# Graph layer 0 of a two-layer network: the order of two copies on ACT, the last tile's own rows, and the order of the last two tiles on DVE

## The reference

```python
h  = maximum(layernorm(x), 0)
xp = (h @ W).reshape(N, 4, 256)                 # with a_src, a_dst: one score per node and head
e  = leaky_relu(a_src[src] + a_dst[dst], 0.2)   # edges and self loops
ee = exp(e - segment_max(e, dst)[dst]); z = segment_sum(ee, dst)
out = segment_sum(xp[src] * (ee / z[dst]), dst)
x  = x + relu(out + bias)
h  = maximum(layernorm(x), 0)                   # the input of layer 1, and its two scores al, ar
```

## Time and profile before

| what | value |
|---|---|
| time, median of 3 runs | 2076.7 us (2073.75 to 2079.98) |
| time of the profiled execution | 2076.24 us |
| its span, first to last instruction | 2074.9 us (1.3 us less) |
| mean granted PE clock | 0.834 of full |
| busy: PE, DVE, ACT, POOL | 79%, 55%, 19%, 70% |
| gathers of `attend` (line 928), landing, min/median/max | 4.2/6.9/13.1 us |

### The profile page before, as it was taken

One profiled execution on the slowest core, in us unless ns is written; L12 is line 12 of the kernel. 1 busy time (PEld: TensorE's weight loads), 2 busy tenths in 40 slices (PEclk: granted clock), 3 DMA queues, 4 the chain that ended last, 5 costly groups with the idle time before them and its releaser, 6 DMA issues. The chain is left out here.

```text
span 2074.9 us, 27577 instructions
## 1 busy us (share of the span) xinstructions
PE 1642.4 (79%) x10226; PEld 913.5 (44%) x10226; DVE 1137.7 (55%) x2762; ACT 400.0 (19%) x766; POOL 1454.1 (70%) x1331
## 2 busy tenths in 40 slices
PE   5882998896067779787688787853799999999995
PEld 2441444442044445454444444531355555555554
DVE  4874777875026666676666666662344334443331
ACT  2220221211011212212122122111222222222221
POOL 3687888787677777777777777605777777777730
PEclk9996999998557677676777777766799999999998
DMA  6331323321399999999999999727999999999961
GB/s 212 101 91 34 87 80 113 97 79 54 134 357 303 337 335 346 353 321 327 350 338 345 337 340 352 262 76 293 408 409 409 410 409 409 407 410 407 406 227 46
DMA packets 187999, 560.54 MB, mean 270 GB/s; under 512 B 46439, under 2 KB 51252, under 8 KB 187604
## 3 DMA queue, kind: packets, MB, share of 16 engines
q0 software_dynamic: 140832, 416.41, 54.8%
q1 hardware_dynamic: 43428, 129.15, 18.9%
q10 hardware_dynamic: 3600, 13.16, 1.6%
HBM read 553.70 MB, written 53.27 MB: 293 GB/s over the span
## 5 line engine op out<-in xcount | busy, mean ns | idle before, releaser
L928 POOL DMA_INDIRECT ring<-layer_rows,idx x360 | 390.7, 1085 | 122.2 <-issue 106.2
L1494 POOL DMA_INDIRECT ring<-layer_rows,idx x360 | 361.9, 1005 | 116.6 <-issue 108.5
L414 POOL DMA_INDIRECT src_lists<-pay_T,slot_T x266 | 336.5, 1265 | 95.5 <-issue 83.8
L510 PE MATMUL mm<-w_sb,hT 128*128 128x512 f32 x800 | 360.1, 609 | 0.0
L1060 PE MATMUL acc<-ring,weight 128*32 128x256 f32 (+1 forms) x3600 | 331.0, 488 | 5.3 <-DVE weight L1167 5.2
L510 PEld LDWEIGHTS mm<-w_sb,hT 128*128 128x128 f32 x800 | 155.4, 197 | 187.4 <-issue 187.4
L1556 PE MATMUL acc<-ring,weight 128*32 128x512 f32 x1600 | 202.4, 625 | 35.4 <-ACT weight L1504 35.4
L1011 PE MATMUL turned<-ident,edge_a 128*16 128x128 f32 (+1 forms) x125 | 39.8, 319 | 217.6 <-ACT score_T L953 144.3
L1060 PEld LDWEIGHTS acc<-ring,weight 128*32 128x32 f32 (+1 forms) x3600 | 149.4, 138 | 127.6 <-issue 86.4
L1132 DVE TENSOR_REDUCE highest<-wide 128x4 f32<-128x512 f32 x125 | 86.2, 690 | 172.6 <-PE wide L1027 170.6
L1589 PE MATMUL mm_l<-w_high,hT_high 128*128 128x512 f32 x400 | 165.7, 414 | 1.8 <-DVE y L1664 1.8
(11 more groups left out here) (233 smaller groups left out, 2277.0 us busy)
## 6 DMA issues: line engine op xcount, KB each, us to landing
layer_rows<-row_l ACTq DMA_DIRECT2D x25, 514.0 KB, 3.7
layer_rows<-row_l SPq DMA_DIRECT2D x25, 514.0 KB, 7.2
own<-layer_rows SPq DMA_DIRECT2D x25, 512.0 KB, 8.8
x<-xb SPq DMA_DIRECT2D x25, 512.0 KB, 6.3
x1t<-x SPq DMA_DIRECT2D x25, 512.0 KB, 9.3
xt<-in_x_dram SPq DMA_DIRECT2D x24, 512.0 KB, 5.2
xb<-in_x_dram SPq DMA_DIRECT2D x24, 512.0 KB
out_dram<-y SPq DMA_DIRECT2D x24, 512.0 KB
```

The source lines that it names most:

```text
L414: pool.indirect_dma_start(out=list_d, out_offset=bass.IndirectOffsetOnAxis(ap=slot_T[:, b:b + 1], axis=0), in_=pay_T[:, b:b + 1], in_offse ...
L510: last = pe.matmul(mm[k][:, f * HALF:(f + 1) * HALF], hT[k][:, c, :], w_sb[:, c, f * HALF:(f + 1) * HALF], start=c == 0, stop=c == KC - 1)
L928: pool.indirect_dma_start(out=ring[:, t % 2, blocks(c), :][:, q, :], out_offset=None, in_=table0, in_offset=bass.IndirectOffsetOnAxis(ap=i ...
L1494: pool.indirect_dma_start(out=fetched(t, c)[:, q, :], out_offset=None, in_=table1, in_offset=bass.IndirectOffsetOnAxis(ap=idx, axis=0), bo ...
```

## The change

On ACT, `keep_edges(t+1, 4)` and `keep_scores(t+1, 3)` come ahead of `deviate(t-1)`. On DVE, `highest_of(t+1, 3)` comes ahead of `spread_of(t-1)`. The own rows of tile 24 are loaded into the first block of the ring half that tile 23 has used, with a semaphore of their own, when PE has used all of tile 23; SP waits for that and issues the load ahead of the two stores of tile 23. Behind the weights of tile 24 the order on DVE is written out anew for the tiles 23 and 24.

```diff
+        def own_of(t):
+            return own[:, :] if t < TILES - 1 else ring[:, (t - 1) % 2, 0, 0:D]
...
             def load_rows(t):
-                if t >= 1:
+                if t == TILES - 1:
+                    sp.wait_ge(ring_free, RC * t)
+                elif t >= 1:
                     sp.wait_ge(scored, 2 * t)
...
-                sp.dma_start(own[:, :], rows(table0, t)[:, 0:D]).then_inc(own_in, 16)
+                sp.dma_start(own_of(t), rows(table0, t)[:, 0:D]).then_inc(own_in if t < TILES - 1 else own_last_in, 16)
...
             for t in range(TILES):
                 if t + 3 < TILES:
                     load_places(t + 3)
+                if t == TILES - 2:
+                    load_rows(t + 1)
                 store(t)
-                if t + 1 < TILES:
+                if t + 1 < TILES - 1:
                     load_rows(t + 1)
...
                     keep_scores(t + 1, 2)
-                if t >= 1:
-                    deviate(t - 1)
-                if t + 1 < TILES:
                     keep_edges(t + 1, 4)
                     keep_scores(t + 1, 3)
                 if t >= 1:
+                    deviate(t - 1)
                     normalise(t - 1)
...
                 weigh(t)
+                if not more:
+                    break
                 if t >= 1:
                     add_own(t - 1)
...
                 if t >= 1:
                     divide(t - 1)
                     finish(t - 1)
-                if more:
-                    highest_of(t + 1, 2)
+                highest_of(t + 1, 2)
+                highest_of(t + 1, 3)
                 if t >= 1:
                     spread_of(t - 1)
-                if more:
-                    highest_of(t + 1, 3)
-                if t >= 1:
                     score_next(t - 1, 0)
-                if more:
-                    highest_of(t + 1, 4)
-                    find_terms(t + 1)
+                highest_of(t + 1, 4)
+                find_terms(t + 1)
...
+            add_own(TILES - 2)
+            divide(TILES - 2)
+            finish(TILES - 2)
+            normaliser(TILES - 1)
             add_own(TILES - 1)
+            spread_of(TILES - 2)
             divide(TILES - 1)
+            for j in range(2):
+                score_next(TILES - 2, j)
             finish(TILES - 1)
             spread_of(TILES - 1)
```

More of the change, by code:

```diff
@@ L799, in attend @@
         own_in = sem("own_in")
+        own_last_in = sem("own_last_in")
         x_in = [sem(f"xb_in{k}") for k in range(2)]
@@ L1181, in add_own @@
             def add_own(t):
-                dve.wait_ge(own_in, 16 * (t + 1))
+                if t < TILES - 1:
+                    dve.wait_ge(own_in, 16 * (t + 1))
+                else:
+                    dve.wait_ge(own_last_in, 16)
                 dve.wait_ge(ring_free, RC * (t + 1))
@@ L1185, in add_own @@
                     cols = slice(h * C, (h + 1) * C)
-                    one = dve.scalar_tensor_tensor(out=own[:, cols], in0=own[:, cols], scalar=self_w[t % 2][:, h:h + 1],
+                    one = dve.scalar_tensor_tensor(out=own_of(t)[:, cols], in0=own_of(t)[:, cols], scalar=self_w[t % 2][:, h:h + 1],
                                                    in1=acc[t % 2][:, h, :], op0=ALU.mult, op1=ALU.add)
@@ L1192, in divide @@
                     cols = slice(h * C, (h + 1) * C)
-                    then(dve.scalar_tensor_tensor(out=own[:, cols], in0=own[:, cols], scalar=rz[t % 2][:, h:h + 1],
+                    then(dve.scalar_tensor_tensor(out=own_of(t)[:, cols], in0=own_of(t)[:, cols], scalar=rz[t % 2][:, h:h + 1],
                                                   in1=bias_bc[:, cols], op0=ALU.mult, op1=ALU.add), math)
@@ L1198, in finish @@
                 dve.wait_ge(x_in[k], 16 * (t // 2 + 1))
-                then(dve.scalar_tensor_tensor(out=xt[k][:, :], in0=own[:, :], scalar=0.0, in1=xt[k][:, :],
+                then(dve.scalar_tensor_tensor(out=xt[k][:, :], in0=own_of(t), scalar=0.0, in1=xt[k][:, :],
                                               op0=ALU.max, op1=ALU.add), x1_done)
@@ L1215, in score_next @@
                 to = (al[:, t:t + 1], row[:, D:D + 1])[j]
-                then(dve.tensor_tensor_reduce(out=own[:, 0:HALF].bitcast(BF16), in0=row[:, 0:D], in1=va_bc[:, j, :],
+                then(dve.tensor_tensor_reduce(out=own_of(t)[:, 0:HALF].bitcast(BF16), in0=row[:, 0:D], in1=va_bc[:, j, :],
                                               scale=1.0, scalar=0.0, op0=ALU.mult, op1=ALU.add, accum_out=to), scored)
@@ L1248, in _ @@
                 weigh(t)
+                if not more:
+                    break
                 if t >= 1:
                     add_own(t - 1)
-                if more:
-                    highest_of(t + 1, 0)
+                highest_of(t + 1, 0)
                 normaliser(t)
-                if more:
-                    mark(t + 1)
-                    highest_of(t + 1, 1)
+                mark(t + 1)
+                highest_of(t + 1, 1)
                 if t >= 1:
```

## The result

The changed kernel takes 2101.86 us in the median (2097.25 to 2106.41, 4 runs) against 2078.34 us for the kernel before (2073.75 to 2082.09, 4 runs): ratio 1.0106, interval 1.0083 to 1.0129. The forecast was 2077, with a range up to 2086. The profiled execution took 2104.46 us with a span of 2102.7, 27.8 more than before.

A forecast was written before the change was run, and what follows sets the result against it. DMA transfers were taken to bound the body, then PE and DVE: -5.7 (end) + 3.0 (passes 22, 23) + 3 (body) = +0.3 on 2076.24, 2076.5; with 0.5 for the runs' median 2077.0. Range, 8 in 10: 2070.5 to 2086.

The forecast's parts named there:

- the +3 us for the body: Passes 2 to 21: POOL's added waits beyond 1 us a pass, 4.5 us, less the shorter queue's return.
- the transfers set the pace: In the body of attend, until about 1320 us, DMA at 1.00 is the bound; PE, ACT and DVE follow.
- work in hand: In the body, DMA engines have some us of queued transfers, since gathers land 6.9 us after issue in the median.
- a shorter queue gives something back: In the body, fewer queued transfers shorten the landing, taking the 4.5 us of counted waits down to +3.
- The size of the stall: Each pass, PE idles about 2.4 us between widen 3 and widen 4, through a new chain over DVE and ACT.
- rival (c): Slower: transfers run dry in the body, all 12.6 us come through, worsened by PE's clock: +9.9, 2086.6; chance 0.32.
- all 12.6 us of waits: Passes 2 to 21: upper bound on POOL's added waits for PE at group 3's gather, if none is covered.
- The copies: On ACT, group 4's edge copy was early in 22 of 23 passes; moving it gains only 1.85 us, in pass 23.
- Pass 22 and 23: At the end, 2.3 us later in pass 22, then -1.85 + 2.5 in pass 23: +3.0 us in all.
- The tiles 23 and 24 on DVE: The new end order brings the last score to 1394.3 against 1399.98, before the stall's shift: -5.7 us.
- add_own(24) waits for PE, not for the rows: At the end, tile 24's own rows, asked for around 1370, arrive before PE ends at 1379.57; a quiet load took 5.40 us.
- rival (d): At the end, tile 23's row store lands late: +3.5 us, 2080.5; chance counted within the 0.55 for "same".

The follow-up runs named there:

- e16: Kernel before with ten tiny iotas added on POOL between the gathers of groups 1 and 2 of tiles 2 to 23, no transfer more: ratio 1.0226.
- e13: Kernel before without the loads of x from the third tile on: ratio 0.9971.
- e7: Kernel before, all orders old, with twenty repeats of a matmul on PE ahead of the last widen: ratio 1.0275.
- e8: Kernel before with only the move on DVE (highest_of 3 ahead of spread_of): ratio 1.0116.
- e6: Kernel before, all orders old, with ten repeats of a matmul on PE ahead of the last widen: ratio 1.0069.
- e5: Changed kernel with the first matmul of the last widen repeated nine times more on PE, from the second pass on: ratio 1.0042.
- e3: Kernel before with only the move on ACT (copies of group 4's edges and group 3's scores ahead of the deviation): ratio 0.9983.
- e2: Changed kernel with both moves on ACT and DVE undone, keeping the own rows' load and new end order: ratio 0.9958, 2071.42 us.
- e14: Changed kernel with only the move on DVE undone, keeping the move on ACT and the new end: ratio 0.9971.
- e11: Changed kernel run again with nothing altered, as yardstick on another chip, against the kernel before: ratio 1.0109.

## Why the prediction was wrong

**The step that failed** is the +3 us for the body, and under it the first reading, that "the transfers set the pace". From it came the belief that the DMA engines have work in hand which covers POOL's waits, and that a shorter queue gives something back. The term was also worked out from the idle time alone, with nothing for the clock (next paragraph). The runs showed three things in place of the cover. POOL sets the pass of 32.0 us by issuing without a break (e16, e13), so what it waits is nearly all lost: at group 3 it waited 31.1 us more than before, and the body lost 26.0. The queue gave back what I had seen in it, but little: the mean gather on POOL took 1065 ns instead of 1084, some 7 us over 360 gathers. And F, from the issue to the landing, was 15.8 to 17.2 us in the runs with all transfers in which POOL waited for PE, and not shorter for the longer waits. The pass is then the longer of two: POOL's 32.0 us, or F + E + 0.3, the loop from a gather through PE back to the same group's next gather. Before, that loop had 2.0 us of slack in the mean; the change added 3.8 to E and took 0.5 from F. The rule is exact to 0.1 us in the changed kernel, e7 and e8; where long and short passes mix, the measured pass is longer by up to 1.2 (e6).

**The size of the stall.** The prediction had 2.4 us for the new idle time; it is 2.13 in pass 17 and 2.35 in pass 9, and over the passes the last widen starts 2.5 us later behind the landing (9.0 to 11.5). That term was right. But E grew by 3.8 us, from 13.3 to 17.1. The rest is the clock: the last spread up to the start of add_rows takes 0.7 us more, add_rows itself 0.6 more (3.0 to 3.6 in the mean). The prediction named the clock in its rival (c) and put it at nothing in the sum. The rule of the Trainium skill beside that rival ("TensorE: Matmul & The Clock Gate", HAM oscillation, that idle gaps throw the clock back) was the right warning, and the trace agrees where the level fell across the gap, in 12 of the 20 passes. Filling the gap (e5) took 2.2 us off E and 60% of the loss off the time. That is more than the gap's clock had cost, since the repeats also kept add_rows at the high level where it had been low before.

**Rival (c)** is what happened, with its mechanism in another form: not the transfers run dry, POOL does. Its upper bound, all 12.6 us of waits, had been worked out with a stall of 2.4 us. By the same formula, with the spacings read in the prediction, a delay of 3.8 gives max(0, 4.1 - pair) in each pass, about 36 us at the most; 31.1 us were added at group 3 (35.0 - 3.9).

**The copies.** Right: the copy of group 4 had been early in 22 of 23 passes, and in e3 the pass stayed the same.

**Pass 22 and 23.** Pass 22 added 2.2 us, as predicted (2.3). Pass 23 added 4.2 instead of 0.7. The wait of 1.85 us went, but PE then waited 1.5 us for highest_of 2 and 2.1 for the scores, and the clock fell again.

**The tiles 23 and 24 on DVE.** Predicted -5.7 us, measured -5.4 in the changed kernel and -5.5 in e2. add_own of tile 24 starts 0.3 us behind PE's last matmul (1404.87 + 7.26 = 1412.13), close to what was worked out:

```profile
1402.69 2.02 DVE L1196 SCALAR_TENSOR_TENSOR own<-own,self_w,acc 128x256 f32<-128x256 f32 x4
...
1412.44 2.03 DVE L1196 SCALAR_TENSOR_TENSOR ring<-ring,self_w,acc 128x256 f32<-128x256 f32 x4 [1.86 <-DMA ring<-layer_rows]
...
1426.88 0.08 DVE L1226 DVE_READ_ACCUMULATOR2_ANT row_l<- 128x1 f32 x1
```

The profile names the load of the own rows as releaser there, but by little: in e14, where it names PE, the same step took 0.15 us. In e2 and e11 the load came last clearly. In e2:

```profile
1369.14 0.32 SPq L865 DMA_DIRECT2D ring<-layer_rows  x1
...
1372.56 7.26 PE L1069 MATMUL acc<-ring,weight 128*32 128x256 f32 x112
...
1381.39 2.03 DVE L1198 SCALAR_TENSOR_TENSOR ring<-ring,self_w,acc 128x256 f32<-128x256 f32 x4 [1.80 <-DMA ring<-layer_rows]
```

add_own starts 1.57 us behind PE's last matmul (1.53 in e11), some 12 us behind the issue of the load, against 4.9 for the load in the quiet end before (1383.43 to 1388.36). So the prediction's "add_own(24) waits for PE, not for the rows" held in the changed kernel only by luck, all but a tie, and its reading of one quiet load did not carry over; whether an earlier load wins these 1.5 us, no run shows. The row's store of tile 23 was not late (landed 3.12 us behind its issue), so rival (d) did not come up.

**What the trace of before would have told.** The window of 32 us showed POOL busy 25 us and DMA at 1.00, and I took the fuller one for the bound. POOL's groups, with their "issue" time of 0.3 us ahead of each instruction, fill 595 of 600 us. Even the earlier trace rows has it: 24.98 us busy in 24 instructions, each with 0.3 us of issue ahead, is 32.2 of 32 us. The only idle time of POOL that could be saved was the 6 us that it waited for PE.

## What to carry to other kernels

Before a delay is called hidden, find the loop that closes over it: the time from freeing a buffer, through the transfer and the engines, to freeing the same buffer in the next round, against the period. Here it had 2.0 us of slack and the reorder lengthened it by 3.3. An engine that issues transfers is full when its busy and issue times together fill the window, even if a busy share of 78% and a DMA share of 1.00 stand on the page. And when a finishing step is moved behind a scoring step on one engine, look at what stands behind it on the others: one line on DVE tied PE to ACT's normalise.

## What the runs showed of the hardware

Behind an idle gap of 2.1 to 2.35 us PE's last spread ran at the low clock level in 20 of 20 passes (2.07 us in place of 1.15). In 12 of them the spread ahead of the gap had run at the high level; in 8 the level was low already. With the gap filled by repeats of a matmul, the last spread ran at the high level in 18 of 20. A gap is not the only thing that a fall follows: before the change add_rows was low behind a high spread in 11 of 16 passes, with no idle time right ahead. POOL needs about 1.07 us and 0.3 us of issue for each gather of 128 rows, 1084 ns before, 1065 in the changed kernel and, without the x loads, 1085: neither a fuller nor an emptier set of DMA engines changed it much. And a DMA share of 1.00 did not mean that the DMA engines were the bound: with 0.5 MB a pass less it fell to 0.97, and the pass stayed the same.
